# A graph network on one core: seven of 53 edge blocks take another way through the edge stage

## The chip, the cores and the metric

The kernel runs on one core of one Trainium2 chip. The metric is device time in microseconds (us). The core has five engines with a queue each: TensorE (PE; its weight loads are listed as PEld), VectorE (DVE), ScalarE (ACT), GpSimd (POOL) and SyncE (SP), which only issues transfers. Sixteen DMA engines move data; indirect transfers (gathers and scatters by an index) are issued by POOL, the plain ones by SP.

## The reference

The graph has N = 12,500 nodes and E = 200,000 edges, with 64 features on each node and edge. Edges are sorted by `dst`; `src` is random. There are three rounds over the edges:

```python
h = relu(layernorm(x))
h1 = relu(mean over edges by dst of h[src] @ W1l.T + b1 + h @ W1r.T)      # conv1
x = x + (mean by dst of h1[src] @ W2l.T + b2 + h1 @ W2r.T)                # conv2
h = relu(layernorm(x))
msg = relu(concat(h[src], h[dst], edge_attr) @ W1 + b1) @ W2 + b2         # per edge
x = x + mean over edges by src of msg                                     # edge stage
```

The edge stage groups by `src`, by which the edges are not sorted. The product with `W1` is split in three: `h[src] @ W1[:64]` and `h[dst] @ W1[64:128]` are made per node in advance (`parts` and `b_table`), and `edge_attr @ W1[128:]` per edge.

## The kernel before, in words

The 200,000 edges are cut into NB = 53 blocks of BE = 3,840, the last short. For each block conv1 sorts its edges by `src`: the nodes form SRC_WINDOWS = 49 windows of 256, a block has 128 slots for each window (SLOTS = 6,272), and the sort says which slot an edge takes (`place`), and which source and destination a slot has (`slot_rows`, `slot_src`, `slot_dst`). The stages run one behind the other, each in a block of its own with all engines met at its end: `setup`, `project` "conv1_in", `conv` "conv1", `add_missed`, `project` "conv2_in", `conv` "conv2", `add_missed`, `second_norm`, `project` "edge_in", `sum_edges` (the edge stage), `add_missed`, `project` "edge_out". The `add_missed` stages do nothing unless an edge found no slot.

`project` makes node tables in 14 groups; PE transposes and multiplies, ACT and DVE split the result into three bf16 parts, SP stores it (L624). In the convs POOL gathers table rows for each block (L969, ten a block), SP loads slot rows spread over the partitions (L926), in conv1 after storing that block's row and awaiting the store (L815). conv2 also clears the ring `sorted` that the edge stage scatters into (L934).

`sum_edges` is what the change concerns. It is a pipeline over slots of work, NG = 7 to a block, in one written-out order for all engines (`in_turn`). Two things happen in a slot.

- A **part** (ES = 5 a block, 6 tiles of 128 edges each, 261 in all): SP loads attribute rows, a window of `b_table` and destination rows (L1336, L1341, L1345). PE transposes the attributes (L1406), ACT copies them back (L1479), DVE compares destinations (L1586), PE adds attribute products (L1417, f32) and destination products (L1422, bf16) in `rows_ps`, ACT copies them into one of five `rows` buffers (L1487), and POOL scatters its six tiles to their slots in `sorted` (L1388). A `rows` buffer is free when the six scatters from it have landed.
- A **group** (7 windows of one block placed two blocks earlier): SP loads slot rows and the sorted rows `edges` (L1360, L1363). DVE and ACT make the two halves of a one-hot matrix (L1608; L1512, L1519). PE expands source parts into `a_ps` (`expand`, L1435, 42 matmuls). DVE adds `edges` (L1614). A slot later ACT and DVE apply the relu and split the sum in three bf16 parts (L1494, L1619, L1499, L1632), DVE makes a second one-hot matrix (L148), and yet a slot later PE sums per source node (`sum_up`, L1450, 42 matmuls) and DVE adds to `acc` (L1640).

ACT copies `src_of` once for each block (L1535), which marks where a block begins. The ring holds RB = 2 blocks. PE's loop body is one block, that of the other engines two.

## Time and profile before

| | |
|---|---|
| time, median of 3 runs | 4372.72 us (4372.36, 4372.72, 4398.48) |
| span of the profiled execution | 4375.3 us |
| PE busy | 3697.5 us, 85% |
| DVE busy | 3679.1 us, 84% |
| ACT busy | 2589.0 us, 59% |
| POOL busy | 3032.7 us, 69% |
| DMA | 557.42 MB, mean 127 GB/s |
| mean granted TensorE clock | 0.949 |

The profiled execution has no time of its own beside its span; the sums are made against the span. Busy shares are averages over stages with different limits. The stages, by the timeline: setup and conv1_in to 120 us, conv1 to 1290, conv2_in 1297 to 1346, conv2 from there to 2145, second norm 2164 to 2203, edge_in 2203 to 2255, edge stage 2256 to 4330, edge_out to the end.

### The profile page before, as it was taken

How to read it: one execution, taken by the hardware profiler on the slowest of the kernel's cores; microseconds unless marked ns; L12 is line 12 of the kernel's file. 1: busy time of each engine (PE TensorE's matmuls, PEld its weight loads, DVE VectorE, ACT ScalarE, POOL GpSimd, SP SyncE). 2: the span in 40 equal slices, each digit the busy share in tenths (PEclk: the TensorE clock that was granted, in tenths of full speed). 3: DMA queues.
4: the chain of work that ended last, by engine and by line, in shares of the span. 5: the costliest groups of instructions: out<-in, count | busy, mean ns of one | idle time of the engine just before them, and what ended most of it. 6: DMA issues, size and time to landing. Idle time of an engine off the chain costs nothing. (4 is left out here: it accounts for less than half of the span.)

```text
span 4375.3 us, 174335 instructions
## 1 busy us (share of the span) xinstructions
PE 3697.5 (85%) x64703; PEld 3536.1 (81%) x64703; DVE 3679.1 (84%) x6413; ACT 2589.0 (59%) x5168; POOL 3032.7 (69%) x2760
## 2 busy tenths in 40 slices
PE   3699999999977999999758888888888888888876
PEld 3688888888877999999747887877788887788876
DVE  7799999999988888888758888887878878888876
ACT  3455555555545666666537666666666666666664
POOL 1688888888854666666517777777777777777771
PEclk9899999999999999999868999999999999999998
DMA  5233333333326545555335555555555555555552
GB/s 104 68 84 83 83 82 83 83 83 85 82 64 170 118 118 118 118 118 119 68 110 162 163 169 175 174 159 159 164 166 174 174 162 161 160 165 174 174 153 65
DMA packets 481209, 557.42 MB, mean 127 GB/s; under 512 B 180610, under 2 KB 437873, under 8 KB 480870
## 3 DMA queue, kind: packets, MB, share of 16 engines
q1 hardware_dynamic: 395782, 451.91, 36.7%
q0 software_dynamic: 84032, 103.47, 10.2%
q8 instruction: 82, 1.34, 0.1%
q10 hardware_dynamic: 1266, 0.31, 0.0%
q14 instruction: 47, 0.39, 0.0%
HBM read 478.48 MB, written 76.90 MB: 127 GB/s over the span
## 5 line engine op out<-in xcount | busy, mean ns | idle before, releaser
L1388 POOL DMA_INDIRECT sorted_edges<-edge_rows,edge_index x1566 | 1535.3, 980 | 568.0 <-issue 559.1
L969 POOL DMA_INDIRECT conv_got<-parts_table,conv_index x1060 | 1324.5, 1250 | 467.2 <-issue 235.7
L1079 ACT CAST conv_rows<-conv_rows_ps 128x384 bf16<-128x384 f32 x2226 | 1020.3, 458 | 671.4 <-PE conv_rows_ps L993 654.8
L993 PE MATMUL conv_rows_ps<-parts,conv_hot_t 128*128 128x192 bf16 x8268 | 1049.8, 246 | 72.4 <-DVE conv_hot_t L1145 72.4
L1010 PE MATMUL conv_sums<-conv_rows,conv_hot_d 128*128 128x193 bf16 (+1 forms) x8268 | 1052.6, 247 | 3.0 <-DMA conv_got<-parts_table,conv_index 3.0
L993 PEld LDWEIGHTS conv_rows_ps<-parts,conv_hot_t 128*128 128x128 bf16 x8268 | 696.4, 97 | 94.7 <-issue 55.4
L1450 PE MATMUL edge_sums<-edge_parts,edge_hot 128*128 128x64 bf16 (+1 forms) x15582 | 597.2, 200 | 201.0 <-DVE acc L1640 196.7
L1450 PEld LDWEIGHTS edge_sums<-edge_parts,edge_hot 128*128 128x128 bf16 x15582 | 556.8, 102 | 220.9 <-DVE acc L1640 165.0
L1010 PEld LDWEIGHTS conv_sums<-conv_rows,conv_hot_d 128*128 128x128 bf16 x8268 | 720.4, 98 | 4.2 <-DMA conv_got<-parts_table,conv_index 3.7
L1435 PE MATMUL edge_a_ps<-parts,edge_hot_t 128*128 128x64 bf16 x15582 | 548.7, 197 | 36.4 <-issue 25.3
L1145 DVE TENSOR_SCALAR conv_hot_t<-conv_slot_row,node_of 128x768 bf16<-128x768 bf16 (+1 forms) x1484 | 542.1, 407 | 22.0 <-PE conv_rows_ps L993 14.6
L1435 PEld LDWEIGHTS edge_a_ps<-parts,edge_hot_t 128*128 128x128 bf16 x15582 | 514.4, 101 | 39.0 <-issue 27.9
L1417 PE MATMUL edge_rows_ps<-edge_attr_w,edge_attr_t 128*128 128x64 f32 x3132 | 406.8, 282 | 141.7 <-ACT edge_rows L1487 140.9
L1417 PEld LDWEIGHTS edge_rows_ps<-edge_attr_w,edge_attr_t 128*128 128x128 f32 x3132 | 389.7, 200 | 159.4 <-issue 143.1
L148 DVE TENSOR_TENSOR conv_hot_d<-conv_nodes_ps,conv_dst_of 128x1792 bf16<-128x1792 bf16 x371 | 403.2, 1087 | 90.8 <-PE conv_sums L1010 90.7
L148 DVE TENSOR_TENSOR conv_hot_d<-nodes_b,conv_dst_of 128x1792 bf16<-128x1792 bf16 x371 | 401.6, 1082 | 57.4 <-PE conv_sums L1010 57.3
L1614 DVE TENSOR_TENSOR edge_a_ps<-edge_a_ps,edge_edges 128x448 f32<-128x448 f32 x371 | 234.0, 631 | 243.4 <-PE edge_a_ps L1435 232.2
L1640 DVE TENSOR_TENSOR acc<-acc,edge_sums 128x455 f32<-128x455 f32 x742 | 429.3, 621 | 0.5 <-PE edge_sums L1450 0.5
L1487 ACT COPY edge_rows<-edge_rows_ps 128x384 f32<-128x384 f32 x261 | 125.3, 480 | 480.4 <-DMA sorted_edges<-edge_rows,edge_index 474.8
L148 DVE TENSOR_TENSOR edge_hot<-edge_nodes_ps,edge_src_of 128x1792 bf16<-128x1792 bf16 x371 | 400.5, 1079 | 0.0
L1512 ACT ACTIVATE edge_distance<-edge_slot_row,edge_minus_node 128x896 bf16<-128x896 bf16 x371 | 389.1, 1049 | 8.9 <-DMA edge_slot_row<-slot_rows 8.9
L1519 ACT ACTIVATE edge_hot_t<-edge_distance,edge_one 128x896 bf16<-128x896 bf16 x371 | 389.0, 1048 | 0.0
(193 smaller groups left out, 4717.5 us busy)
## 6 DMA issues: line engine op xcount, KB each, us to landing
edge_slot_row<-slot_rows SPq DMA_DIRECT2D x371, 224.0 KB
edge_edges<-sorted_edges SPq DMA_DIRECT2D x371, 224.0 KB
conv_slot_row<-slot_rows SPq DMA_DIRECT2D x424, 192.0 KB
conv_slot_row<-slot_rows SPq DMA_DIRECT2D x318, 160.0 KB
edge_dst_row<-dst_rows SPq DMA_DIRECT2D x261, 192.0 KB
edge_attr<-in_edge_attr SPq DMA_DIRECT2D x260, 192.0 KB
sorted_edges<-edge_rows,edge_index POOLq DMA_INDIRECT x1566
conv_got<-parts_table,conv_index POOLq DMA_INDIRECT x1060
```

Source lines behind the costliest of these rows:

```text
L148: return dve.tensor_tensor(hot[:].rearrange("p u (n q) -> p u n q", q=QUAD), wide(quads(nodes), 1, shape), wide(number[:, GU * g:GU * (g + ...
L969: pool.indirect_dma_start(got[g][:, f, 0:PARTS * D], None, k.parts_table, bass.IndirectOffsetOnAxis(ap=index[h][:, g, at:at + 1], axis=0)) ...
L993: mm = pe.matmul(rows_ps[(bs * h + i) % banks][:, at:at + PARTS * D], hot_t[home[g]][:, v, u * P:(u + 1) * P], k.parts[:, 2 * (GU * g + u) ...
L1010: mm = pe.matmul(sums[h][:, v * wide_cols:(v + 1) * wide_cols], hot_d[home[g]][:, u, v * P:(v + 1) * P], row, start=(i == 0 and u == 0 and ...
L1079: act.copy(rows[i % bufs][:, 0:n, 0:PARTS * D], rows_ps[(bs * h + i) % banks][:, 0:n * PARTS * D].rearrange("p (u d) -> p u d", u=n)).then ...
L1145: last = dve.tensor_scalar(hot_t[hot][:, v, 0:n_cols], slot_row[lane[g]][:, 0:n_cols], k.node_of[:, v:v + 1], None, ALU.is_equal)
L1388: pool.indirect_dma_start(k.sorted, bass.IndirectOffsetOnAxis(ap=index[h][0:used, at:at + 1], axis=0), rows[j][0:used, t, :], None).then_i ...
L1417: pe.matmul(rows_ps[:, t, :], attr_t[to][:, t // 2, :], k.edge_attr_w[:, t % 2, :], start=(t == 0), stop=False, skip_group_check=True)
L1435: mm = pe.matmul(a_ps[at][:, u, :], hot_t[at][:, v, u * P:(u + 1) * P], k.parts[:, 2 * (GU * j + u) + v, i, :], start=(v == 0 and i == 0), ...
L1450: mm = pe.matmul(to[:, 0:n], hot[at][:, u, v * P:(v + 1) * P], parts[at][:, u, i, 0:n], start=(i == 0), stop=(i == PARTS - 1), skip_group_ ...
L1512: act.activation(distance[:], slot_row[g][:], ACT.Square, bias=minus_node[:]).then_inc(distant, 1)
L1640: dve.tensor_tensor(part, part, sums[half][:, 0:GU * D1].rearrange("p (w d) -> p w d", d=D1), ALU.add).then_inc(added, 1)
```

## The change

Seven blocks, numbers 45 to 51 (FIRST_EARLY = 45), are "early". Their raw attribute rows are loaded (SP) and scattered (POOL) to their slots in a buffer of their own, `early_sorted`, in the stages from conv2_in to edge_in: 54 tiles in conv2_in, 2 after each of 50 blocks of conv2, 18 in the second norm, and the remaining 38 in edge_in, which waits until all have landed. conv1 clears that buffer. In the edge stage they have no parts: for an early group PE transposes the seven windows of `edges` (4 transposes), ACT copies them back to `early_t`, DVE makes two more one-hot halves from the slots' destinations (`early_hot`), and `expand` adds destination and attribute products to the source products; DVE adds nothing. The order is a start of three items (early block, last block, block 0), then a loop of ROUNDS = 6 rounds of 8 items, the third of each early, with 35 parts spread over the 56 slots, and two last items. The ring of sorted rows grows from 2 to 7 blocks (28 pieces of zeros in conv2, one after each block's loads, for 8 at its start). conv2's loops on SP and POOL are written out.

```diff
+EARLY, ROUND, ROUNDS, AHEAD, STARTED, EARLY_AT = 7, 7, 6, 3, 4, 2
+NORMAL, FIRST_EARLY, RB = NB - EARLY, FULL - EARLY, ROUND
+EARLY_BUFS, BETWEEN, AFTER = 4, 9, 3
+ZE = 112
 class Early:
+    def load(self, eng, upto):
+        while self.loaded < min(upto, EARLY * ES):
+            c, r = self.loaded, self.loaded % EARLY_BUFS
+            if c >= EARLY_BUFS:
+                eng.wait_ge(self.k.early_scattered[r], 16 * ET * (c // EARLY_BUFS))
+            at = (ES * FIRST_EARLY + c) * P
+            eng.dma_start(self.rows[r][:], self.attr[at:at + P]).then_inc(self.k.early_landed[r], 16)
+            self.loaded += 1
+    def scatter(self, pool, tiles):
+        for _ in range(tiles):
...
+            if t == 0:
+                pool.wait_ge(self.k.early_landed[r], 16 * (c // EARLY_BUFS + 1))
+            pool.indirect_dma_start(self.k.early_sorted, bass.IndirectOffsetOnAxis(ap=self.index[:, at:at + 1], axis=0),
+                                    self.rows[r][:, t, :], None).then_inc(self.k.early_scattered[r], 16)
 def project(...):                                   # conv2_in: early=BETWEEN; edge_in: early=EARLY * ES
+                k.early.scatter(pool, early * ET - k.early.tiles)
+                if early == EARLY * ES:
+                    k.early.wait_all(pool)
+                for g in range(2, last - 1):
+                    k.early.load(sp, first + (g - 1) * GROUPS // (GROUPS - 1) * 3 // 4)
+                    body(g, g % 2, g // 2, MANY)
 def conv(...):
+            def clear_early(e):
+                to = k.early_sorted[bass.ds(RING_ROWS * e, SLOTS), :].rearrange("(p r) d -> p (r d)", p=P)
+                n = SLOTS // P * D // ZE
+                sp.dma_start(to.rearrange("p (n c) -> p n c", c=ZE), wide(zero[:], 1, [P, n, ZE])).then_inc(zeros_stored, 16)
+                with sp.Fori(1, 1 + EARLY) as b:     # conv1
+                    load(b, MANY)
+                    clear_early(b - 1)
+                for b in range(1, NB):               # conv2, SP
+                    load(b, MANY)
+                    if b <= pieces:
+                        sp.dma_start(to[:, (b - 1) * ZC:b * ZC], zero[:]).then_inc(zeros_stored, 16)
+                    if b % 3 == 0:
+                        k.early.load(sp, BETWEEN + EARLY_BUFS + (b // 3 - 2))
+                for b in range(2, NB - 1):           # conv2, POOL
+                    fetch(b, b % 2, MANY)
+                    k.early.scatter(pool, 2)
 def second_norm(...):
+            k.early.scatter(pool, AFTER * ET)
 def sum_edges(...):
+            starts = {1 + p * long // (ROUND * ES): p for p in range(ROUND * ES)}
+            with eng.Fori(0, ROUNDS) as i:
+                for s in range(long):
+                    slot(...)
 # SP
+                if group.early and g < EARLY_ROWS:
+                    early_row(group.index, g)
+                if before is not None and before.early and g + EARLY_ROWS < NG:
+                    sp.wait_ge(early_hot_made, before.done)
+                    early_row(before.index, g + EARLY_ROWS)
 # PE: turn(next part), products(part), sum_up(two back), early_turn(ahead), expand(now)
+            def turn(part, now):
...
+                if now is not None and now.early:
+                    pe.wait_ge(early_ready, now.done)
+            def early_turn(group, part):
+                pe.wait_ge(edges_landed[group.g], 16 * (group.item + 1))
+                pe.wait_ge(attr_ready, part.q + 1)
+                wait_positive(pe, early_ready, group.done - 1)
+                for i in range(QUAD):
+                    u = min(2 * i, GU - 2)
+                    mm = pe.transpose(attr_ps[:, i, :], edges[group.g][:, u:u + 2, :].rearrange("p u d -> p (u d)"), k.ident[:])
             def expand(group):
+                if group.early:
...
+                    pe.wait_ge(early_hot_made, group.done)
+                    pe.wait_ge(early_ready, group.done)
...
+                    if group.early:
+                        for v in range(2):
+                            for i in range(PARTS):
+                                pe.matmul(a_ps[at][:, u, :], early_hot[:, v, u * P:(u + 1) * P], early_b[:, v, i * D:(i + 1) * D], start=False, stop=False)
+                        half = u % 2 if u < GU - 1 else 1
+                        mm = pe.matmul(a_ps[at][:, u, :], early_t[:, u // 2, :], k.edge_attr_w[:, half, :], start=False, stop=True)
 # ACT, at the end of a slot
+            def early_back(group):
+                act.wait_ge(early_turned, group.done)
+                if group.g:
+                    act.wait_ge(expanded, group.number + NG)
+                act.copy(early_t[:], attr_ps[:]).then_inc(early_ready, 1)
 # DVE, at the end of a slot
+            def make_early_hot(group):
...
+                if g:
+                    dve.wait_ge(expanded, group.number + NG)
+                for v in range(2):
+                    made = dve.tensor_scalar(early_hot[:, v, :], early_dst[r][:], k.node_of[:, v:v + 1], None, ALU.is_equal)
+                made.then_inc(early_hot_made, 1)
```

## Rows read from the trace of the kernel before

**Rows 1.** Waits, edge stage 2500 to 4200 us: who for whom, total us, times, longest.
```profile
ACT edge_rows L1487 <- DMA sorted_edges<-edge_rows,edge_index: 441.7, 160, 4.7
POOL sorted_edges L1388 <- issue: 401.2, 1315, 0.3
```

**Rows 2.** Windows: length, busy PE, PEld, DVE, ACT, POOL (instructions), clock, DMA share, GB/s.
```profile
2377.30:2409.20 31.90, 29.27 (x758) 28.91 (x756) 30.92 (x56) 24.68 (x41) 24.27 (x26) 1.00 0.49 141
...
2500.00:2700.00 200.00, 166.71 (x3902) 162.57 (x3899) 160.47 (x284) 125.88 (x202) 152.41 (x157) 0.92 0.53 161
```

**Rows 3.** Timeline of ACT, the copy that begins a block: start, length.
```profile
2307.29 0.34 ACT L1535 COPY edge_src_of<-slot_src 128x196 bf16<-128x196 bf16 x1
2344.80 0.34 ACT L1535 COPY edge_src_of<-slot_src 128x196 bf16<-128x196 bf16 x1
...
2409.19 0.34 ACT L1535 COPY edge_src_of<-slot_src 128x196 bf16 x1
...
4292.30 0.34 ACT L1535 COPY edge_src_of<-slot_src 128x196 bf16<-128x196 bf16 x1
```

**Rows 4.** Timeline of PE, a slot with a part, and one without.
```profile
2349.36 0.53 PE L1406 MATMUL edge_attr_ps<-ident,edge_attr 128*128 128x128 f32 x3
2349.72 1.45 PE L1417 MATMUL edge_rows_ps<-edge_attr_w,edge_attr_t 128*128 128x64 f32 x12
2351.01 0.69 PE L1422 MATMUL edge_rows_ps<-edge_b_win,edge_hot_b 128*128 128x64 bf16 x18
2351.53 1.48 PE L1450 MATMUL edge_sums<-edge_parts,edge_hot 128*128 128x65 bf16 x42
2352.86 1.39 PE L1435 MATMUL edge_a_ps<-parts,edge_hot_t 128*128 128x64 bf16 x42
2354.08 0.53 PE L1406 MATMUL edge_attr_ps<-ident,edge_attr 128*128 128x128 f32 x3
...
2374.59 1.57 PE L1450 MATMUL edge_sums<-edge_parts,edge_hot 128*128 128x65 bf16 x42 [1.66 <-DVE acc L1640]
```

**Rows 5.** Groups by line, whole span: busy us, mean ns | idle before.
```profile
L1608 DVE TENSOR_SCALAR edge_hot_t<-edge_slot_row,node_of 128x896 bf16<-128x896 bf16 x371 | 173.3, 467 | 8.4 <-DMA edge_slot_row<-slot_rows 8.4
...
L587 ACT ACTIVATE conv_in_h_t<-conv_in_turn_ps 128x512 f32<-128x512 f32 x28 | 16.7, 597 | 39.4 <-PE conv_in_turn_ps L560 38.7
```

**Rows 6.** Timeline, the edge stage's first load and last addition.
```profile
2255.70 0.32 SPq L1331 DMA_DIRECT2D edge_attr<-in_edge_attr  x1
...
4328.43 1.29 DVE L1640 TENSOR_TENSOR acc<-acc,edge_sums 128x455 f32<-128x455 f32 x2 [0.46 <-PE edge_sums L1450]
```

**Rows 7.** Timeline of POOL, conv2, the first gathers of two blocks.
```profile
1696.69 1.09 POOL L969 DMA_INDIRECT conv_got<-parts_table,conv_index  x1 [2.45 <-ACT conv_index L1094]
...
1711.69 1.05 POOL L969 DMA_INDIRECT conv_got<-parts_table,conv_index  x1 [2.47 <-ACT conv_index L1094]
```

**Rows 8.** Timeline of SP, first loads of conv2_in and of conv2.
```profile
1297.02 1.58 SPq L615 DMA_DIRECT2D conv_in_both_w<-conv_w  x2
...
1347.18 3.20 SPq L926 DMA_DIRECT2D conv_slot_row<-slot_rows  x7
```

**Rows 9.** Timeline, second norm's POOL work, and SP at edge_in's start.
```profile
2163.72 15.79 POOL L1841 TENSOR_TENSOR own_part<-acc,inv_count 128x896 f32<-128x896 f32 x7 [20.03 <-PEq L1822]
...
2203.17 2.44 SPq L615 DMA_DIRECT2D edge_in_both_w<-in_L_gnn_W  x4
```

**Rows 10.** Timeline, conv1: slot row stored, loaded for group 0, used.
```profile
313.27 0.32 SPq L815 DMA_DIRECT2D slot_rows<-conv_slot_row  x1
315.14 0.34 SPq L926 DMA_DIRECT2D conv_slot_row<-slot_rows  x1
...
321.21 0.82 DVE L1145 TENSOR_SCALAR conv_hot_t<-conv_slot_row,node_of 128x768 bf16<-128x768 bf16 x2
```

**Rows 11.** Window in edge_in, while b_table is stored (columns of rows 2).
```profile
2228.00:2238.00 10.00, 7.02 (x40) 5.88 (x39) 7.66 (x14) 5.52 (x11) 0.00 (x0) 1.00 0.49 136
```

**Rows 12.** DMA queues, whole span: packets, MB, share of 16 engines.
```profile
q8 instruction: 82, 1.34, 0.1%
```

644 lines of the change are left out of this document (375 added, 269 removed).

## The prediction

> **What bounds the kernel now.** I read the page's slices first (three long stages: conv1, conv2, edge stage), then the waits of the edge stage's steady part, then windows, single slots and stage edges. The edge stage is paced by GpSimd. In 1,700 us ScalarE waits 441.7 us for scatters to land before it may overwrite a `rows` buffer, while POOL waits for nothing but its own 0.305 us between two scatters (401.2 us over 1315) [rows 1]. A scatter is busy 0.971 us (152.41/157) [rows 2], so POOL's cadence is 1.276 us, 38.3 us for the 30 scatters of a block. The blocks come 38.43 us apart (2409.19 to 4292.30, 49 blocks) [rows 3]. The reader is to see that nothing else needs so long: just after the start, while the buffers were still empty, three blocks came after 32.5, 31.9 and 33.1 us, the first two being the 64.4 us from 2344.80 to 2409.19 [rows 3], at a granted clock of 1.00 against 0.92 later [rows 2]. That is the compute pace: a slot with a part takes 4.72 us with PE never idle (transposes 0.36, attribute products 1.29, destination products 0.52, sums 1.33, expansion 1.22), a slot without one 4.4 to 4.5 us, in which PE waits for VectorE [rows 4].
>
> **The change, part by part.** I sum against the profiled execution, whose span is 4375.3 us; the median of the runs, 4372.7, is 2.6 lower. The last addition of the edge stage ends at 4329.7, its first load was at 2255.7 [rows 6]: 2074 us.
>
> *Edge stage, what goes.* 210 of 1566 scatters, 35 parts of 261: POOL's work falls by 210 x 1.276 = 268 us. With them go their loads, PE's 2.17 us per part, VectorE's and ScalarE's share. POOL now needs 35 x 6 x 1.276 = 268 us for a round of 8 items, where 8 blocks took 8 x 38.43 = 307 us; at the measured pace (38.43 per 30) it is 269 us.
>
> *Edge stage, what comes.* An early group has 42 more bf16 products (priced like the expansion, 1.22), 7 f32 products (1.29/12 each, 0.75) and 4 transposes (0.36/3 each, 0.48): 2.45 us of PE. VectorE drops the addition of rows (0.6) and makes two compares of 128x896 (0.47 each); ScalarE copies 128x512 back, 0.60 us by the nearest row of that size [rows 5]. The buffers `early_t`, `early_hot` and `attr_ps` are single: ScalarE's and VectorE's work for the next group starts only when PE's expansion has ended, and PE's next transposes of a part wait for that copy, about 0.75 us with the handover. Queued behind that wait on PE are the part's products and the sums of two groups back; behind ScalarE's wait stands its first copy of the present group, which releases VectorE. SP's queue gets eight more loads in an early item (seven compare rows, one window of the table); the later four rows wait for a compare of VectorE one item back, which the load behind them waits for in kind already, so I cost them at nothing: their cover is that SP runs an item ahead, and without it each would show its landing, about 2 us. The same cover hides the ring: the last part of a round is scattered up to five parts (38 us, eight slots) behind, as its first reader comes up. An early slot with a part so costs 4.72 + 2.45 + 0.75 = 7.9 us, without one 2.55 + 2.45 = 5.0, call it 5.1. Four of the seven early slots of a round have a part: 46.9 us.
>
> *A round.* Of the other 49 slots 31 have a part: 31 x 4.72 + 18 x 4.45 = 226.4. With the early item 273.3 us, which is above POOL's 269, so PE and VectorE set it, though barely. Bounds: below, POOL's 269 (spread parts could let slots with and without one average out, since PE needs 2.55 in one and 4.72 in the other); above, 292, if the clock falls to the 0.92 of [rows 2] whenever PE pauses (6% of 273 is 16) and the ring's waits add a few us. I take 276, nearer to the dense window with its clock of 1.00. What is late next after ScalarE's stall is gone: VectorE's additions in slots without a part, and PE in early ones.
>
> *The stage.* Lead to the first group 51.6 (2255.7 to 2307.3), early item 44 (three parts fall in it), 5 more for the cold clock (the first block took 37.5, not 32.5) [rows 3], items 1 and 2 with 7 parts 64, six rounds 1656, the last two items without parts 14 x 4.45 = 62, drain 6. Together 1889, against 2074: **-185 us**.
>
> *conv2's preparation.* 54 scatters at 1.276 are 69 us, begun about 3 us into a stage that lasts from 1297 to 1346 [rows 8]. The stage's end waits for POOL: about 1369, **+24** (bounds 18 and 30; the first pieces must be loaded, and SP, which waits for a scatter before each later load, stores table rows behind it until about 1360, still ahead of POOL). The tables made for the early blocks (compares, transposes, copies, stores) lie beside this.
>
> *conv2.* A block takes 15.0 us. POOL's ten gathers fill 12.5 of them and it then waits 2.47 us for the next index [rows 7]. Two scatters take 2.55 us, and the next gather's own 0.3 follows: 15.4. Over 50 blocks POOL slips 20 us; a gather is issued about 10 us before PE uses its rows (issued 1696.7, landed about two later, its group's sums near 1710), which hides half: **+10** (bounds 0 and 28). Zeros for seven ring blocks go out one piece per block, and 17 loads of attribute rows, all on SP, which waits most of a block, so nothing; the burst of zeros at its start goes.
>
> *conv1.* After each of blocks 1 to 7 SP issues a clear of 1.6 MB in pieces of 448 bytes, ahead of the store of the slot row, whose landing SP awaits before loading the next; I take transfers of one queue to land in order. The store now takes 1.87 us (313.27 to 315.14), and the load of group 0 is out 6.1 us before its use at 321.21 [rows 10]; with about 2.5 to land, 3.6 us are spare. Rows of 384 bytes moved at 136 GB/s with the DMA engines 49% busy [rows 11], so 1.6 MB takes 5.8 us of all engines, some 7 beside other traffic: about 3 us of stall seven times, **+20** (bounds 0 and 50, the upper one with nothing spare). The Trainium skill, page DMA: Bandwidth & Descriptors, section Specifications, says pieces under 512 bytes are read, modified and written; were the rate half, the sum would have about 40 more. The row of 384-byte pieces shows no such loss, and no run so far shows 448.
>
> *Second norm and edge_in.* 18 scatters (23 us) after POOL's tensor work end at 2202.6, where the stage ends at 2203.2; the last 38 (48.5) and their landing (2) end near 2255, the stage at 2255 [rows 9]: **+3** (0 to 8). Setup's sixth and seventh small DMA: nothing, beside x's loads.
>
> Sum: -185 + 24 + 10 + 20 + 3 = -128, so 4247 in the profiled execution and **4245 us** as a median.
>
> **Rivals.**
> *A, POOL still paces.* For it: its 269 is only 4 below my 273. Then 6 x 269 gives -42 more, and with cheap side stages (30 in all instead of 57) the time is about 4175. 14%.
> *B, the early item costs more.* Its chain over three engines stands in no row. Each extra us in an early slot costs 7 x 6.5 = 46 us: at 1 to 2 us more, 4290 to 4335. 14%, with the clears at their upper bound as the other way there.
> *C, PE starves for instructions, and the kernel is slower.* The place is PE's loop: one block of 753 matmuls and as many weight loads becomes a body of about 6,230 of each. All code fetched on queue 8 is 1.34 MB in 82 packets of 16 KB [rows 12]; by my count of the program PE's code is some 21,000 instructions, each fetched about once, 250 to a packet, though 129,000 ran. So the small loop was hardly fetched again; the large one may be each round. If each 16 KB held PE up, 12,460/250, some 49 of them, a round, the gain of 128 is gone at 128/(6 x 49) = 0.44 us each; at 1 us each the time is about 4410 and at 1.3 us 4500, over 1% slower. Against it: the blocks at 2344 to 2409 are straight code, passed once, and PE ran their slots back to back [rows 4]. 9% slower than before by over 1%, and part of the 13% for no change. The Trainium skill, page Runtime: NRT & Kernel Launch, section Instruction fetch mechanics, says PE holds 2,048 instructions, the next are fetched ahead in sequence, and a taken branch out of the window stalls. By that the old loop fits and the new one does not, and only the branches back would cost, six in all; the trace's straight code agrees as far as it goes.
> *D, nothing moves:* rounds of 297 us (276 + 128/6), by B and C in part. 13%.
>
> **How the numbers follow.** My forecast (4200 to 4290) has 50%. A and B take 14% each, D 13%, C 9%. The range 4160 to 4350 leaves out C (9%), two thirds of D (8%) and A's tail (3%). 1% is 44 us, about what a measurement of this kernel can tell from no change. Faster than 4329: 0.50 + 0.14 + most of B = 0.77; within: 0.14; slower: 0.09.
>
> **What the changed profile would show.** Right: ScalarE's wait for scatters falls from 442 us per 1,700 to under 100; rounds of 270 to 284 us; PE over 85% busy at a clock above 0.95; POOL's issue gap no longer its only wait; conv2's preparation 20 to 30 us longer and paced by POOL; conv2's POOL without its 2.5 us wait. Wrong: "issue" gaps on PE in the edge loop; an early item over 55 us; VectorE in conv1 waiting over 6 us for a slot row; conv2's blocks at 15.4 us from the first on.

## The result: 1.1% faster, a third of what was forecast

The changed kernel takes 4336.05 us (median of 4 runs, 4321.41 to 4353.98) against 4385.1 for the kernel before on the same chips (4 runs, 4372.36 to 4398.48): ratio 0.9894, 95% interval 0.9847 to 0.9942. A later comparison on one chip gave 0.9919 (0.9891 to 0.9948). The forecast was 4245, with a range from 4160 to 4350. The span of the profiled execution is 4343.2 against 4375.3, 32.1 less, where the sum had 128. Stage by stage, each from its first issue to that of the next stage:

| stage | before | after | change | forecast |
|---|---|---|---|---|
| conv1 and all ahead of it (to 1297.02, 1326.74) | 1297.0 | 1326.7 | +29.7 | +20 |
| conv2_in | 50.2 | 82.9 | +32.8 | +24 |
| conv2 | 816.5 | 832.1 | +15.5 | +10 |
| second norm and edge_in | 92.0 | 102.2 | +10.2 | +3 |
| edge stage, first load to last addition | 2074.0 | 1938.3 | -135.7 | -185 |
| edge_out, to the end of the span | 45.6 | 61.0 | +15.4 | 0 |

The page of the changed kernel:

```profile
PE 3751.1 (86%) x66492; PEld 3578.1 (82%) x66492; DVE 3668.2 (84%) x6427; ACT 2597.8 (60%) x5151; POOL 3029.2 (70%) x2761
...
q8 instruction: 378, 6.19, 0.6%
```

The second line answers to [rows 12]: 296 packets of code more. The prediction's count for a PE loop body that is fetched anew in every round was 6 x 49 = 294. The row does not say which engine's code they are; 313 packets of the 378 fall between 2515 and 4215 us, in the rounds.

In the edge stage the stall of [rows 1] is gone. The waits of the six rounds (2515 to 4215 us; engine and line, what for; us in total, times, longest):

```profile
POOL sorted_edges L1581 <- issue: 361.6, 1186, 0.3
POOL sorted_edges L1581 <- ACT edge_rows L1695: 105.1, 36, 8.4
PE edge_sums L1662 <- DVE acc L1862: 96.6, 109, 1.0
PE edge_attr_ps L1599 <- issue: 24.9, 5, 5.6
PE edge_attr_ps L1599 <- ACT edge_early_t L1735: 17.9, 26, 0.7
...
SPq L1395 <- DMA sorted_edges<-edge_rows,edge_index: 169.9, 29, 14.6
```

ScalarE waits for no scatter, but POOL now waits 105.1 us for rows: it runs dry in the early items. PE has five gaps without a releaser, one at each branch back. And SyncE, which loads sorted rows ahead of the groups, waits 169.9 us for scatters to land (the last line): in every round it stands at the seventh and eighth item and at the next round's first, waiting for the last parts of a round (experiment 5). The starts of the items (ScalarE's copy of `src_of`) give their lengths, in us:

| round | items | sum |
|---|---|---|
| 1 | 32.0 31.8 **51.4** 34.9 30.5 30.8 31.0 35.8 | 278.2 |
| 2 | 39.0 32.5 **51.7** 34.8 30.3 31.8 33.6 37.2 | 290.9 |
| 3 to 6 | early items 51.2, 51.5, 51.2, 52.0 | 279.4, 282.0, 285.9, 283.3 |

Rounds take 283.3 on average, forecast 276; the items at a round's end and start mostly 33 to 39 where the fifth to seventh take 31.1 on average. The early item by this mark is 51.5. But ScalarE's mark comes a slot ahead of PE: the last of the seven early expansions falls in the next item, which is why that one takes 34.8 or 34.9 every time. From the first slot with an early expansion to the end of the seventh PE takes 55.8 to 56.6 us, mean 56.0, where the forecast was 46.9. Inside an early slot, PE's timeline (start, us, operation, idle before it):

```profile
2581.75 0.63 PE L1624 MATMUL edge_attr_ps<-ident,edge_edges 128*128 128x128 f32 x4
2582.22 0.34 PE L1641 MATMUL edge_a_ps<-parts,edge_hot_t 128*128 128x64 bf16 x6
2582.39 0.34 PE L1646 MATMUL edge_a_ps<-edge_early_b,edge_early_hot 128*128 128x64 bf16 x6
2582.56 0.41 PE L1648 MATMUL edge_a_ps<-edge_attr_w,edge_early_t 128*128 128x64 f32 x2
...
2595.34 0.55 PE L1599 MATMUL edge_attr_ps<-ident,edge_attr 128*128 128x128 f32 x3 [0.73 <-ACT edge_early_t L1735]
```

The reader is to see the x2: one f32 product is two instructions, and each window takes 0.60 us (2582.22 to 2582.82), of which 0.26 is the attribute product. Seven make 4.2 us. With nothing of a part in it an early slot takes 5.99 us (seen in experiment 3, where such slots are many). In the changed kernel a part's transposes and its products often stand in different slots: an early slot takes 7.3 us with the transposes, 7.9 with the products and 9.1 with both. Now the first branch back, on PE, and the granted clock around it:

```profile
2791.12 0.67 PE L1641 MATMUL edge_a_ps<-parts,edge_hot_t 128*128 128x64 bf16 x17 [1.18 <-issue]
2797.13 0.90 PE L1599 MATMUL edge_attr_ps<-ident,edge_attr 128*128 128x128 f32 x3 [5.34 <-issue]
2797.82 2.49 PE L1662 MATMUL edge_sums<-edge_parts,edge_hot 128*128 128x65 bf16 x42
```

```profile
2791.00:2797.10 6.10, 0.67 (x17) 0.55 (x17) 1.70 (x3) 0.81 (x2) 4.75 (x5) 0.63 0.70 206
2797.10:2807.50 10.40, 8.47 (x121) 8.26 (x122) 5.77 (x12) 4.64 (x7) 7.79 (x9) 0.56 0.44 154
```

In the windows the columns are the length, busy time (instructions) of PE, PEld, DVE, ACT, POOL, granted clock, DMA share and GB/s. PE stands still for 5.3 us, and for the 10.4 us behind it runs at a clock of 0.56, mostly the lower level of 1.2 GHz (42 sums take 2.49 instead of 1.48).

The stages ahead, by SyncE's issues in conv1 (a block with a clear) and the two ends of conv2_in:

```profile
296.42 16.17 SPq L1044 DMA_DIRECT2D conv_slot_row<-slot_rows  x7
312.80 0.60 SPq L1050 DMA_DIRECT2D early_sorted<-conv_zero  x1
314.01 3.91 SPq L933 DMA_DIRECT2D slot_rows<-conv_slot_row  x1
321.68 16.17 SPq L1044 DMA_DIRECT2D conv_slot_row<-slot_rows  x7
...
1326.74 2.11 SPq L720 DMA_DIRECT2D conv_in_both_w<-conv_w  x2
...
1409.68 10.44 SPq L1044 DMA_DIRECT2D conv_slot_row<-slot_rows  x9
```

Behind a clear, the store's issue alone takes 3.91 us instead of 0.32, and the next load follows after 7.7 us instead of the 1.87 of [rows 10]; this block is 25.3 us long instead of 21.4, the others with a clear 24.1 to 26.5. Over the seven the stage is 29.7 us longer, 4.2 each. In conv2_in POOL's first and last scatter, and in conv2 the seam between two blocks:

```profile
1332.40 1.01 POOL L510 DMA_INDIRECT early_sorted<-early_rows,early_index  x1 [28.54 <-DMA early_rows<-in_edge_attr]
...
1403.98 0.97 POOL L510 DMA_INDIRECT early_sorted<-early_rows,early_index  x1 [0.30 <-issue]
```

```profile
1701.58 1.06 POOL L1100 DMA_INDIRECT conv_got<-parts_table,conv_index  x1 [0.30 <-issue]
1702.95 1.00 POOL L510 DMA_INDIRECT early_sorted<-early_rows,early_index  x1 [0.30 <-issue]
...
1705.54 1.01 POOL L1100 DMA_INDIRECT conv_got<-parts_table,conv_index  x1 [0.30 <-issue]
```

POOL begins 5.7 us into conv2_in, needs 72.6 us for 54 scatters (some 20 of them alternate between 1.3 and 1.6 us), and the next stage's first load comes 4.7 us after the last. In conv2 the 2.47 us wait of [rows 7] is gone, and a block is 15.4 us.

The last stage is code that the change does not touch. Its windows, of the changed kernel and then of the kernel before:

```profile
4304.00:4312.00 8.00, 8.00 (x44) 8.00 (x44) 3.34 (x7) 2.26 (x3) 0.00 (x0) 0.55 0.26 67
4312.00:4343.00 31.00, 26.86 (x129) 26.67 (x128) 9.97 (x18) 4.72 (x6) 0.00 (x0) 0.50 0.23 59
```

```profile
4352.00:4360.00 8.00, 7.91 (x72) 7.69 (x72) 4.87 (x10) 2.75 (x4) 0.00 (x0) 1.00 0.36 88
4360.00:4375.00 15.00, 10.64 (x97) 10.39 (x94) 8.43 (x15) 3.65 (x4) 0.00 (x0) 0.95 0.44 106
```

In the changed kernel's trace the granted clock was 1.00 from 4295 to 4304 us, with PE 95% busy, then fell to 0.50, the level of 1.2 GHz, and stayed there; the stage took 61.0 us instead of 45.6. I come back to that at the end. Without it the spans differ by 47.5 us.

### The profile page after: what moved, and what is told of

The parts are those of the page before. It is cut to its first block and busy times, and to the rows that moved or that the text cites. A ratio compares the mean times of both kernels' runs of the same rounds, so it can differ in the third digit from the quotient of the medians.

```text
span 4343.2 us, 176322 instructions
## 1 busy us (share of the span) xinstructions
PE 3751.1 (86%) x66492; PEld 3578.1 (82%) x66492; DVE 3668.2 (84%) x6427; ACT 2597.8 (60%) x5151; POOL 3029.2 (70%) x2761
## 5 line engine op out<-in xcount | busy, mean ns | idle before, releaser
L1581 POOL DMA_INDIRECT sorted_edges<-edge_rows,edge_index x1356 | 1335.8, 985 | 563.0 <-issue 391.7
L1100 POOL DMA_INDIRECT conv_got<-parts_table,conv_index x1060 | 1309.3, 1235 | 388.2 <-issue 247.4
L1662 PE MATMUL edge_sums<-edge_parts,edge_hot 128*128 128x64 bf16 (+1 forms) x15582 | 566.3, 195 | 145.0 <-DVE acc L1862 128.9
L1662 PEld LDWEIGHTS edge_sums<-edge_parts,edge_hot 128*128 128x128 bf16 x15582 | 525.1, 99 | 178.1 <-DVE acc L1862 122.3
L1641 PE MATMUL edge_a_ps<-parts,edge_hot_t 128*128 128x64 bf16 x15582 | 573.9, 194 | 20.0 <-issue 15.4
L1641 PEld LDWEIGHTS edge_a_ps<-parts,edge_hot_t 128*128 128x128 bf16 x15582 | 537.5, 100 | 24.0 <-issue 18.3
L1710 ACT ACTIVATE edge_parts<-edge_a_ps 128x448 bf16<-128x448 f32 x371 | 204.8, 552 | 247.1 <-DVE edge_a_ps L1836 219.9
L1608 PE MATMUL edge_rows_ps<-edge_attr_w,edge_attr_t 128*128 128x64 f32 x2712 | 349.2, 280 | 3.9 <-ACT edge_rows L1695 3.2
L1608 PEld LDWEIGHTS edge_rows_ps<-edge_attr_w,edge_attr_t 128*128 128x128 f32 x2712 | 332.0, 198 | 5.2 <-issue 3.8
L1146 PE MATMUL conv_sums<-conv_got,conv_hot_d 128*128 128x193 bf16 (+1 forms) x2120 | 298.8, 247 | 0.0
```

The lines of the kernel that those rows point to most:

```text
L1100: pool.indirect_dma_start(got[g][:, f, 0:PARTS * D], None, k.parts_table, bass.IndirectOffsetOnAxis(ap=index[h][:, g, at:at + 1], axis=0)) ...
L1146: mm = pe.matmul(sums[h][:, v * wide_cols:(v + 1) * wide_cols], hot_d[home[g]][:, u, v * P:(v + 1) * P], row, start=(i == 0 and u == 0 and ...
L1581: pool.indirect_dma_start(k.sorted, bass.IndirectOffsetOnAxis(ap=index[s.part.ring][0:used, at:at + 1], axis=0), rows[j][0:used, t, :], No ...
L1608: pe.matmul(rows_ps[:, t, :], attr_t[to][:, t // 2, :], k.edge_attr_w[:, t % 2, :], start=(t == 0), stop=False, skip_group_check=True)
L1641: mm = pe.matmul(a_ps[at][:, u, :], hot_t[at][:, v, u * P:(u + 1) * P], k.parts[:, 2 * (GU * g + u) + v, i, :], start=(v == 0 and i == 0), ...
L1662: mm = pe.matmul(to[:, 0:n], hot[at][:, u, v * P:(v + 1) * P], parts[at][:, u, i, 0:n], start=(i == 0), stop=(i == PARTS - 1), skip_group_ ...
```

## The experiments

Times below are medians, and ratios are to the kernel before in the same comparison. Since edge_out varies by itself, the verdicts rest on stages and rounds.

**1. The branch: the loop over rounds written out on every engine.**

```diff
-            with eng.Fori(0, ROUNDS) as i:
+            for i in range(ROUNDS):
...                                 # and two waits that the loop asks for stay
```

> The loop over six rounds is written out on every engine, so that nothing branches back in the edge stage; order and work are the same. Theory 1 (the branch back costs, code in sequence does not): the five gaps of 3.6 to 5.6 us at PE's first transposes of a round go, and with them the 10 us at a granted clock of 0.56 to 0.86 behind each; the items around a round's start fall from 33 to 39 us to 31 to 33, a round from 283 to 274 to 277, the time by 35 to 50 us against the changed kernel. The instruction queue's packets stay near 378. Theory 2 (PE's code is short everywhere since it no longer stays in place, the branch being only where it shows): the gaps named issue spread over the stage and their sum stays near 57 us; no gain over 10 us. Theory 3 (the slow items are the ring of sorted rows, or POOL, at a round's end): items stay at 33 to 39 us and the wait for scatters shows on SP's loads.

4301.81 us, ratio 0.982 (0.9778 to 0.9861). PE's gaps at a round's start are gone, the rounds take 273.4 to 284.3, mean 279.1, and the items at a round's end 31 (31 to 37 with the loop). The instruction queue moved 367 packets, nearly as many as with the loop. So it is the branch back over a body of this size that costs: 4.2 us a round, 25 over the stage. What is left (same window as before):

```profile
PE edge_a_ps L1648 <- issue: 13.8, 18, 1.7
PE edge_sums L1669 <- issue: 11.3, 15, 2.1
SPq L1395 <- DMA sorted_edges<-edge_rows,edge_index: 225.7, 19, 20.3
```

Straight code is not free of gaps on PE: with a third line of 4.0 us these make 29 us in 37 pieces, in stretches in which the DMA engines are about 90% busy (63% over the rounds). The kernel before has as much in its 49 blocks, so that no run here shows whether they are fetches. The saving is less than the 35 to 50 us expected by the rounds (25) and at its edge by the medians (34), and the second item of a round still takes 33 to 37 us from the second round on. The last line points at its cause: in the item before it SyncE stands 16 to 20 us for scatters and then issues its loads in a burst. Experiment 5 bears this out.

**2. The same, PE's loop alone.**

```diff
+            if eng is nc.tensor:
+                for i in range(ROUNDS):
...                                 # else the loop as it was
```

> Only PE's loop over the rounds is written out, the other engines keep theirs. Theory 1 (the gap at the branch is PE's own code being fetched again): PE's five gaps of 3.6 to 5.6 us go as with all engines written out, rounds near 279 us. Theory 2 (ScalarE and VectorE, which also show gaps of 13.7 and 17.9 us in five pieces, have code too long to stay in place as well, and hold PE up): PE now waits for them at a round's start, 3 us or more five times, and rounds stay at 281 to 284.

4307.55 us (one run). PE has no long gap left at the round's start, rounds 281.3, between the two theories: about half of the gain comes from PE's code, the rest with that of the other engines, which have gaps of their own (17.9 and 13.7 us of DVE and ACT in the changed kernel). That these hold PE up is the likely reason, from one run.

**3. Early slots without a part.**

```diff
-            starts = {1 + p * long // (ROUND * ES): p for p in range(ROUND * ES)}
+            free = [s for s in range(1, long) if s // NG != EARLY_AT]
+            starts = {free[p * len(free) // (ROUND * ES)]: p for p in range(ROUND * ES)}
```

> Only the places of the 35 parts in a round change: none falls in the seven early slots, where four stood, and 35 of the other 48 take one. Theory 1 (PE is the bound in an early slot, and pays every part there in full): an early slot without a part takes 5.97 us in the trace after the change, a turn adds 1.46 and products 1.86, while in an ordinary slot a part costs 0.27 (4.72 against 4.45). Four parts moved give 4 x 3.3 = 13.2 less 1.1, so the early item falls from 51.3 to 41.8 to 43 us, the rest of the round grows by 1 to 3, a round falls from 283 to 273 to 276, the time by 40 to 60 us against the changed kernel (about 4285, ratio to the kernel before 0.977 to 0.980). Theory 2 (the chain over ScalarE, VectorE and PE with single buffers bounds the early slot): its length does not depend on the part, the early item stays at 49 us or more, gain under 15 us. Theory 3 (POOL becomes the bound, since it works off at most five buffers, 38 us, in an early item of 42): ScalarE waits for scatters again, over 30 us in the six rounds, and a round stays at 278 or more.

**4393.78 us, ratio 1.0019 (0.9996 to 1.0043)**: all of the gain lost, 58 us against the changed kernel, where theory 1 had 40 to 60 less. In the profile the span is 49 us longer: 31 are the rounds, 6 the rest of the edge stage, and 12 are edge_out (73.0), which varies by itself. The early item did fall, to 41.1 to 45.0, but the items around it rose to 35 to 43 and a round to 288.4. Two of its waits in the six rounds:

```profile
POOL sorted_edges L1582 <- ACT edge_rows L1696: 143.3, 26, 24.9
ACT edge_rows L1696 <- DMA sorted_edges<-edge_rows,edge_index: 54.8, 21, 4.6
```

POOL stands dry for up to 24.9 us in one piece while the early item gives it nothing, and outside it is late: ScalarE waits for scatters again, and SyncE waits 379.8 us for them before it loads edges (169.9 in the changed kernel). Theory 3 held. That made me count POOL's round in the changed kernel: (1699.7 - 105.1)/1260 = 1.266 us a scatter, 266 us of work, plus 17.5 dry, 283. The expectations from here on build on this sum. But POOL is always either scattering or dry, so it comes out for any round whatever sets its length; what POOL costs takes a run with less for it to do (experiment 5).

**4. A backlog ahead of the early item.** Parts in all 13 slots ahead of it, none in it.

```diff
+            first = EARLY_AT * NG - 1
+            starts = {1 + p if p < first else (EARLY_AT + 1) * NG + (p - first) * (long - first - NG - 1) // (ROUND * ES - first): p for p in range(ROUND * ES)}
```

> Places of the 35 parts again: slots 1 to 13 of a round, those ahead of the early item, all take one (13), the seven early slots none, the 35 slots behind them 22. Theory 1 (POOL sets the pace outside the early items and runs dry inside them: 269 us of work for a round plus 17.5 us dry, 105.1 us in six rounds, is 286 against the measured 283; with no part at all in the early item it was dry 24 us a round and a round took 288): POOL enters the early item with four to five buffers to work off, is dry under 40 us in the six rounds instead of 105 and 143, the early item takes 41 to 45 us, the items at a round's end and start 31 to 34 instead of 33 to 43, and a round takes 272 to 277 us: 35 to 65 us less than the changed kernel. Theory 2 (the loss with parts away came from the ring, parts too late for their readers, not from POOL's idle time): SyncE still waits over 300 us for scatters and rounds stay above 283. Theory 3 (PE cannot feed 13 parts in a row; ScalarE waits for buffers): the two items ahead of the early one take over 37 us and eat the gain.

4318.12 us, ratio 0.9864 (0.9829 to 0.9899), rounds 281.2. The waits of ScalarE and POOL:

```profile
ACT edge_rows L1696 <- DMA sorted_edges<-edge_rows,edge_index: 59.8, 22, 4.9
POOL sorted_edges L1582 <- ACT edge_rows L1696: 84.5, 20, 13.5
```

Theory 1 fell (84.5 us dry instead of under 40, rounds of 281.2 instead of 272 to 277), theory 2 too (SyncE's wait for scatters is down to 66.4 us), and theory 3 held for the most part: the early item is 40.8 us and the last item of a round 30 to 35, but the item ahead of the early one takes 41 to 46 us (all five `rows` buffers are full, PE waits), and POOL still runs dry once a round, 11 to 13.5 us at the early item's end. The gain over the changed kernel's rounds is 2 us.

**5. POOL's share alone.** The first of the six scatters of each part is left out, with its rows.

```diff
-                for t in range(ET):
+                for t in range(1, ET):
...                                 # and 5 instead of 6 in every wait for scatters
```

> The changed kernel with one of the six scatters of each part left out, 222 us of POOL's work a round. Theory 1 (POOL and its dry time set part of the 283): a round takes 272 to 279, and what is left of slow items stands at PE's branch. Theory 2 (POOL has no part in it): 281 to 285.

Rounds of 275.9 to 283.8, mean 279.4, where the changed kernel on the same chip had 283.1: theory 1, at its upper end. With POOL relieved PE, VectorE and the branch need 279.4, so POOL's part in the round is 3.7 us, not the 17.5 that it is dry. SyncE's wait for scatters, 169.9 us in the changed kernel, and the second item show where it sat:

```profile
SPq L1395 <- DMA sorted_edges<-edge_rows,edge_index: 29.9, 9, 7.8
```

The second item takes 31 to 33 us here, and 32 to 37.5 in the changed kernel.

**6. The attribute products of the early groups left out.**

```diff
-                        mm = pe.matmul(a_ps[at][:, u, :], early_t[:, u // 2, :], k.edge_attr_w[:, half, :], start=False, stop=True)
```

> The attribute products of the early groups (PE's seven f32 products a slot, 14 instructions in the trace) are left out; transposes, copies and destination products stay. Theory 1 (PE bounds the early slot, and my working had half as many instructions as there are): 1.79 us less of PE per early slot, of which 1.0 to 1.5 show before VectorE (4.7 us busy in such a slot, plus handovers) becomes the bound: the early item falls from 51.3 to 41 to 44 us. Theory 2 (handovers of the single buffers bound it): the early item stays over 47 us.

(The last destination product closes the sum instead.) The early item by ScalarE's mark falls to 44.1 to 46.7, mean 45.1, 6.4 less, the item behind it by 2 (33), and a round to 274.3, 9 less. One early slot of PE, from its transposes to those of the next:

```profile
2591.37 0.63 PE L1624 MATMUL edge_attr_ps<-ident,edge_edges 128*128 128x128 f32 x4
...
2597.50 0.63 PE L1624 MATMUL edge_attr_ps<-ident,edge_edges 128*128 128x128 f32 x4
```

PE does bound the early slot, with a floor close beneath it: a slot with products of a part falls from 7.86 to 6.13 us, by nearly the whole 1.79, the seven together from 56.0 to 47.6, by 8.4 of 12.5. Theory 1 held, though the marked item stayed 1 us above its range.

**7. The clears in four forms**, in one kernel, block after block.

```diff
-                with sp.Fori(1, 1 + EARLY) as b:
-                    load(b, MANY)
-                    clear_early(b - 1)
+                for b in range(1, 8):
+                    load(b, MANY)
+                    if b not in (3, 4):
+                        clear_early(sp, b - 1 if b < 3 else b - 3, ZE if b < 3 else 2 * ZE)
...
+                    if i == 0 and sorting and isinstance(b, int) and b in (8, 9):      # ScalarE's queue
+                        clear_early(act, b - 3, ZE)
```

> conv1's clears take four forms, one after the other: behind blocks 1 and 2 as in the changed kernel (SP's queue, pieces of 448 bytes), behind 3 and 4 none, behind 5, 6 and 7 pieces of 896 bytes from SP, behind 8 and 9 pieces of 448 bytes from ScalarE's queue. Undisturbed a block takes 21.4 us, with a clear 25.3. Theory 1 (the store of the slot row lands behind the clear in its own queue, whatever the size of piece): blocks 1, 2, 5, 6, 7 are each 3.5 to 4.5 us longer, the store is issued and landed in about 7.9 us instead of 1.9; from ScalarE's queue the block is under 1 us longer. Theory 2 (pieces under 512 bytes are slow in themselves): 896-byte clears cost at most half, a block is under 2 us longer, and 448 bytes from the other queue still slow the store. Theory 3 (the DMA engines are shared and full for those 8 us): all forms of clear cost the same 3 to 4 us, whichever queue they are in.

SyncE's issues (L1041 is a clear, L933 the store of the slot row), and one of ScalarE's:

```profile
184.25 0.64 SPq L1041 DMA_DIRECT2D early_sorted<-conv_zero  x1
184.94 4.56 SPq L933 DMA_DIRECT2D slot_rows<-conv_slot_row  x1
192.96 16.02 SPq L1054 DMA_DIRECT2D conv_slot_row<-slot_rows  x7
...
279.42 2.10 SPq L933 DMA_DIRECT2D slot_rows<-conv_slot_row  x1
286.26 15.93 SPq L1054 DMA_DIRECT2D conv_slot_row<-slot_rows  x7
...
349.66 0.33 SPq L933 DMA_DIRECT2D slot_rows<-conv_slot_row  x1
351.53 19.83 SPq L1054 DMA_DIRECT2D conv_slot_row<-slot_rows  x7
```

```profile
338.00 0.67 ACTq L1041 DMA_DIRECT2D early_sorted<-conv_zero  x1
```

From store to next load: 8.0 and 8.4 us with 448-byte pieces, 6.8, 6.6 and 6.7 with 896, 3.0 and 2.3 with no clear, 1.9 and 2.0 with the clear on ScalarE's queue. Windows in the midst of a clear with 448-byte pieces from SyncE, with 896, and with 448 from ScalarE:

```profile
187.00:191.00 4.00, 4.00 (x51) 4.00 (x49) 2.99 (x5) 2.71 (x7) 3.39 (x3) 1.00 1.18 284
281.00:284.00 3.00, 3.00 (x39) 3.00 (x37) 2.79 (x5) 2.30 (x6) 2.39 (x3) 1.00 1.06 367
341.00:345.00 4.00, 4.00 (x79) 3.82 (x76) 4.00 (x9) 1.76 (x4) 2.83 (x1) 1.00 1.18 277
```

A clear fills all DMA engines for some 6 to 7 us, from whichever queue it comes, and moves 277 to 284 GB/s in 448-byte pieces and 367 in 896-byte ones. A store issued right behind it lands when it is over. Theory 1's "whatever the size of piece" fell, and for its queue this shows less than it seems: ScalarE's clear went out at 338.00 and was over by 347, before the store at 349.66 was issued. So the run shows that a clear which is over by then costs the store nothing. Whether one at the store's own time on another queue would cost nothing too (theory 1) or as much (theory 3) it leaves open. Theory 2's rate effect exists, but is worth 1.5 us of 8: the Trainium skill (DMA: Bandwidth & Descriptors, Specifications) has pieces under 512 bytes read, modified and written; if that halved the rate here, the 6.3 us that a clear adds to a store (8.2 less 1.9) would have become about 3.1 with 896-byte pieces; they became 4.8. conv1 as a whole was 15 us longer than in the kernel before, instead of 29.7.

**8. The 210 early scatters left out**, with their rows; loads and clears stay.

```diff
-            pool.indirect_dma_start(self.k.early_sorted, ...).then_inc(self.k.early_scattered[r], 16)
+            pool.sem_inc(self.k.early_scattered[r], 16)
```

> The 210 scatters of raw attribute rows are left out (POOL only counts their semaphores up), their loads and everything else stay; early rows read zeros. Each stage then shows what its scatters cost. Theory (POOL is what lengthens the stages): conv2_in falls from 83 to 50 to 53 us, conv2's period from 15.4 to 15.0 us (15 us over the stage), second norm from 44 to 39 to 40, edge_in from 58 to 52 to 54; conv1 and the edge stage do not change. Rival (loads, table stores and the index in conv2_in are what takes the time): conv2_in stays over 65 us, conv2 stays within 5 us of the changed kernel.

conv2_in 49.8 us (82.9), conv2 816.0 (832.1), second norm 39.4 (44.2), edge_in 52.4 (57.9), conv1 and the rounds (281.9) within 2 us of the changed kernel. The scatters are all that lengthens the four stages: 33.1 + 16.1 + 4.8 + 5.5 = 59.5 us.

**9. Three edits in one**: the dense places of 4, the loop written out, and conv1's clears in 49 pieces of 230 KB, one a block.

```diff
-                n = SLOTS // P * D // ZE
+                n = SLOTS // P * D // ZE // 7            # piece q of clear e, behind block 7 * e + q + 1
```

> Three edits in one: the dense places, every engine's loop over rounds written out, and conv1's clears cut in 49 pieces of 230 KB, one behind each of 49 blocks, instead of seven of 1.6 MB. If the parts add up: conv1 as long as in the kernel before (27 to 30 us back, since a piece of a seventh of 8 us fits in the 3.6 us a store has to spare), rounds of 268 to 273 us (POOL's 269 is the floor) against 283, hence 4215 to 4250 us. If POOL's pace is the floor already with the dense places, writing out the loop adds nothing to them (rounds within 2 us of those of the dense kernel), and the time is 4245 to 4265. If the pieces in conv1 still hold up the store each by over a us beyond its spare time, conv1 gives back under 15 us.

4284.56 us, ratio 0.9773 (0.9737 to 0.9809). conv1 ends at 1294.68, 2.3 ahead of the kernel before: all of the 29.7 us are back. Rounds are 280.2 instead of the 268 to 273 of my sum, so the loop written out added 1 us a round to the dense places, where it gave 4.2 to the spread ones, and the time is above both its ranges (edge_out 72.2 in the profile). That the two edits would not add up in the rounds was the second theory, but the rounds lie above POOL's floor.

**10. One and two parts put back into the early item.** A first run of both, and of 5, fell on a chip on which the kernel before took 6221.56 us (both 2.8% and 3.2% slower than it there, with gaps between single matmuls and late loads throughout); I take nothing on the rounds from it. The second:

```diff
+            ahead = [*range(1, EARLY_AT * NG)] + [19]         # the other kernel: + [18, 20]
+            rest, after = ROUND * ES - len(ahead), (EARLY_AT + 1) * NG
+            starts = {at: p for p, at in enumerate(ahead + [after + n * (long - after) // rest for n in range(rest)])}
```

> The kernel with one part in the early item once more, since the first three-kernel comparison ran on a chip on which the kernel before took 6221 us instead of 4374, most of it in late loads and in gaps named issue, so that nothing there tells of POOL's dry time. Theory (POOL's 266 to 270 us plus its dry time make the round): dry 3 to 5 us a round, rounds of 272 to 276 against 280 with none in the early item. Rival (PE, VectorE and their buffers set the round): 281 to 284.

> Two parts in the early item. By the theory POOL is not dry, PE needs 275.6, rounds of 273 to 277, within 3 us of the kernel with one. By the rival 284 and more.

4296.7 (ratio 0.983, 0.9796 to 0.9864) and 4285.93 us (0.9811, 0.9785 to 0.9836); rounds 280.9 and 280.0, against 280.2 with none. My theory fell in this form; the rival's 281 to 284 fits the kernel with one part, its 284 and more not the one with two. The early item rose by some 4 us a part (40.1, 44.7, 48.4), other items fell by as much, and POOL was hardly less dry (80, 75 and 68 us over the six rounds). Of the kernel with two:

```profile
POOL sorted_edges L1591 <- ACT edge_rows L1705: 61.8, 24, 7.0
ACT edge_rows L1705 <- DMA sorted_edges<-edge_rows,edge_index: 49.7, 19, 5.1
```

The changed kernel itself ran beside them:

> The changed kernel itself, as it is, beside the three on the same chip: rounds of 283 us and a time of 4320 to 4355 us, if this chip is as the first ones.

4332.7 us, rounds 283.1, edge_out 45.8: as forecast.

**11. Parts neither in a burst nor in the early item's way**: slot 1, slots 5 to 13, two in the early item, 23 behind.

```diff
+            ahead = [1, *range(5, EARLY_AT * NG), 16, 19]
```

> Loop written out and clears in 49 pieces as before; of a round's parts one stands in slot 1, nine in slots 5 to 13, two in the early item (its third and sixth slot) and 23 behind it. With 13 ahead of the early item the buffers were full there (PE held 8 to 10 us in the item ahead of it) and POOL still dry 9 to 10 us a round behind it, in all three kernels of that kind, rounds of 280 to 281. Theory (a queue of five buffers between PE and POOL, both needing 270 to 276 us a round, loses on both sides when the parts come in a burst): PE's item ahead of the early one falls from 40 to 42 to 33 to 35 us, POOL is dry 4 to 7 us a round, a round takes 275 to 278 us, the time 4250 to 4275. Rival (the round is 280 whatever the places, because POOL's scatters slow down when they come closer together): rounds of 279 or more.

**4268.94 us, ratio 0.9762 (0.9727 to 0.9797)**: the fastest of all, 1.5% below the changed kernel's 4332.7 (measured on another chip). Its waits:

```profile
POOL sorted_edges L1591 <- ACT edge_rows L1705: 61.1, 38, 7.1
ACT edge_rows L1705 <- DMA sorted_edges<-edge_rows,edge_index: 1.4, 2, 0.9
```

ScalarE hardly waits for scatters, PE's item ahead of the early one takes 35.5 to 39.8, rounds 274.9 to 281.6, mean 278.3. That is at the theory's edge: against the dense places the burst cost 2 us a round, but POOL is still dry about 13 us a round (78 us over its own six rounds, which begin ahead of the window), and the last two rounds (281.6, 281.0) are no better than before. What holds the item ahead of the early one at 36 to 40 I have not isolated. Against experiment 1, which left the parts where they were and had rounds of 279.1, the new places give less than 1 us: nearly all of what this kernel gains on the changed one comes from the loop written out (about 25 us) and the clears in small pieces (about 31). Those two alone, with the spread places, were not run.

## Why the prediction was right in sign and wrong in size

*What bounds the kernel before* was right: the stall of [rows 1] vanished, PE is 90% busy in the rounds at a clock of 0.98, and the time fell. The gain was 47.5 us short of edge_out, not 128. The step that failed is the price of an early slot, and behind it the side stages were priced too low one by one. The missing 80 us are 49 of the edge stage (44 in the rounds, 5 in the first, cold early item) and 31 of the stages ahead of it:

- **"An early slot so costs 7.9 us with a part and 5.1 without"**, 46.9 for the seven: they take 56.0, which is 9.1 a round and 55 in six rounds, more than all that the edge stage missed. A slot without anything of a part takes 5.99, and a part adds 3.3 (1.3 for its transposes, 1.9 for its products) where 2.8 was taken. The error of 0.9 is in "7 f32 products (1.29/12 each, 0.75)": the row had x12 for six tiles, so one product is two instructions, fourteen here, 1.79 us. Experiment 6 took them out and a round fell by 9. This is rival B: its "1 to 2 us more" an early slot ("4290 to 4335") is what happened, at 1.3 us. It was looked for in a chain over three engines, and it was PE's own work. The bound "an early item over 55 us" was not passed by ScalarE's mark and was by PE's seven slots.
- **The 49 ordinary slots at 226.4**: 227.3 when the seventh early expansion is counted where it belongs, and that is luck. Undisturbed they are cheaper than priced: the fifth to seventh item take 31.1, 217.4 for seven, since a slot with only a part's transposes takes 3.97 and one with only its products 4.45. The ten us between are the items at a round's end and start. The branch, which the sum had not, is 4.2 of them (experiment 1) and POOL 3.7 (experiment 5), not simply added.
- **"The same cover hides the ring"**, a wait put at nothing: SyncE waits 169.9 us for scatters, and experiment 5 shows that this and the rest of POOL's part cost 3.7 us a round. My bound "POOL's 269" compared whole rounds. It missed that POOL and PE are both within 5% of the round, so that POOL runs dry in the early item and is late at the round's end. Rival A's condition (POOL paces) did not come true: with a sixth of its work gone the round lost 1.3%.
- **Rival C** was right in its place and wrong in its price. Packets rose nearly as counted, by 296, but the same number in straight code (experiment 1) cost no such stops: what shows is the branch, 3.6 to 5.6 us at PE five times and a low clock behind it. That a taken branch out of the window stalls and sequential code is fetched ahead, the rule cited there (the Trainium skill, Runtime: NRT & Kernel Launch, Instruction fetch mechanics), agrees with this; the short gaps that straight code keeps are not explained. One sum of this rival was wrong: at 1 us a packet its 6 x 49 packets give 4245 + 294, about 4540 us, not 4410, and at 1.3 us about 4630, not 4500.
- **conv2_in "+24"**: 32.8. The scatters took 72.6 us, not 69, began 5.7 us into the stage, not 3, and 4.7 us pass between the last one and the next stage. The forecast's end of the stage, 1297 + 3 + 69 = 1369, left out the 4.7.
- **conv1 "+20"**: 29.7. Mechanism and place were right (the store lands behind the clear), and so was the rate, 277 GB/s with the DMA engines full; a clear cost 4.2 us instead of 3: its own issue of 0.6 was not counted, and the next load follows 7.7 to 7.9 us after the store's issue, where I had about 7 for the clear.
- **conv2 "+10", second norm and edge_in "+3"**: 15.5 and 10.2. The ten us of lead of a gather were to hide half of POOL's slip of 20 us and hid about a quarter. In the second norm 18 scatters took 26.1 us, not 23, and the next stage's first load comes 2.2 us behind them (4.8 in all); edge_in must wait for the last scatters to land, 5.4 us late.
- **edge_out 0**: +15.4, not the change's doing (below).

Lead (51.7), items 1 and 2 (65.6) and the end of the stage (67.2, forecast 68) came as forecast. Of the signs named, four came true (ScalarE's wait, PE's busy share, POOL's issue gap, conv2's lost wait) and two in part: conv2_in is paced by POOL but 32.8 us longer, not 20 to 30, and the rounds are 270 to 284 on average, but not two of the six. Of the wrong ones two came true: issue gaps on PE, and conv2's blocks at 15.4 us from the first on. VectorE in conv1 waits for a slot row at most 3.9 us.

## What to carry to other kernels

Price an operation by the instructions that its row counts, not by the calls in the code: a factor of two in one f32 product was 6 us a round. Measure an item on the engine that is late in it: a mark on another engine can cut a slot off. An engine's work plus its idle time is always the period; what its work costs the others shows when some of it is taken away (here 3.7 us, where it was dry 17.5). When two engines both need nearly the whole period, compare them stretch by stretch, since moving work out of one stretch can cost more in the next than it saves. A bulk store belongs behind nothing that is awaited: cut it to the slack that is there, or let it go out when nothing is awaited soon.

## What the hardware showed that I had not expected

- **The last stage's clock.** edge_out, the same code in every kernel, took 45 to 46 us in nine profiles (the kernel before among them), 50.5, 61.0, 61.5 and 61.1 in four, and 72.2 and 73.0 in two, the slow chip's three apart. In the traces of 61.0 and 73.0 the granted clock is 0.50 from a point on, with PE 87 to 100% busy, and stays there to the end (in the one of 73.0 from the pause ahead of the stage). A difference of 27 us is also that between the two levels of the kernel before's runs (4366 to 4375 at a mean clock of 0.950, 4395 to 4400 at 0.944); those other runs have no profile, so that this is their cause is likely and not shown. The changed kernel's runs spread from 4321 to 4354; the one of 4344.97 had 61.0 in its profile, the one of 4325.07 45.8.
- **A pause costs twice.** After PE's 5.3 us at the branch the clock was 0.56 for 10.4 us; after the 3.6 us gap of the next round 0.70 for 10 us.
- **One chip ran the kernels 1.42 to 1.50 times slower** (6221.56 us for the kernel before). The two kernels with the loop written out were 3% slower than the one before there and 2% faster elsewhere; the one of experiment 5, which keeps the loop, was 1.3% faster there (6140.75, one run). That straight code leans on fetches that are late on that chip is a guess. Why that chip is slow no run here tells.
